# Attention and routed experts in one kernel: exponential scores of two heads on the two row halves of TensorE, one value bank by 512 queries, three maximum banks, the maxima split on GpSimd, fp32 down products

## The reference, cut to what matters

```python
q = (x @ Wq.T + bq); k = (x @ Wk.T + bk); v = (x @ Wv.T + bv)      # x: 2 x 1024 x 128, 16 heads of 8
scores = einsum('bqhd,bkhd->bhqk', q, k) * attn_scale[0]
scores = where(mask, -inf, scores)   # kept: keys of a later chunk of 64, and of the query's own chunk up to the query
attn = softmax(scores);  x = layernorm(x + (attn @ v) @ Wo.T + bo)
# experts: 32 of hidden size 64, top 6 of the best 4 of 8 groups, and one shared expert of hidden size 128
routed += combine[:, e] * ((silu(x @ gate_e.T) * (x @ up_e.T)) @ down_e.T)
x = layernorm(x + routed + shared)
```

## Time and profile before

| what | value |
|---|---|
| median of 3 runs | 520.54 us (520.14 to 521.09) |
| span of the profiled execution, first to last instruction | 514.3 us |
| what lies around the span, median less span | 6.2 us |
| projections, splits, values of V | 0 to 37.8 us |
| maxima of group 0 to the last maximum (start of L761 of group 7) | 38.9 to 276.2 us |
| first and last exponential product | 69.3 to 312.2 us |
| last value product | 317.4 us |
| first and last down product | 325.5 to 504.3 us |

### The profile page before, as it was taken

One profiled execution on the slowest core, in us unless ns is written; L12 is line 12 of the kernel. 1 busy time (PEld: TensorE's weight loads), 2 busy tenths in 40 slices (PEclk: granted clock), 3 DMA queues, 4 the chain that ended last, 5 costly groups with the idle time before them and its releaser, 6 DMA issues.

```text
span 514.3 us, 8899 instructions
## 1 busy us (share of the span) xinstructions
PE 468.9 (91%) x3212; PEld 259.2 (50%) x3212; DVE 402.1 (78%) x780; ACT 263.1 (51%) x375; POOL 216.8 (42%) x260
## 2 busy tenths in 40 slices
PE   5899799999999999999999997898988898899872
PEld 1474233444434444443434553686765576667651
DVE  7809977788887878788786457699889889968963
ACT  4510035666656676665576766444564464545440
POOL 9100033625345362544413323455644556655561
PEclk9955559999999999999999999899999999999996
DMA  4444110020211203020000000633222253452320
GB/s 138 154 145 134 59 34 15 7 88 20 73 39 31 66 19 83 26 65 32 3 2 3 1 1 2 138 109 92 83 82 82 83 112 96 120 135 83 102 82 20
DMA packets 23340, 34.22 MB, mean 67 GB/s; under 512 B 5121, under 2 KB 13186, under 8 KB 22530
## 3 DMA queue, kind: packets, MB, share of 16 engines
q1 hardware_dynamic: 23106, 33.41, 22.7%
q10 hardware_dynamic: 192, 0.26, 0.2%
HBM read 29.00 MB, written 4.46 MB: 65 GB/s over the span
## 4 chain that ended last, share of the span: by engine, by line
PE 59%; DVE 16%; issue 10%; POOL 10%; ACT 3%; DMA 2%; SPq 1%; DVEq 0%; POOLq 0%; ACTq 0%
PE ps L1082 15%; PE ps L1039 13%; PE ps L1064 12%; POOL hlo L615 8%; DVE mx L758 6%; DVE hh L983 3%; PE ps L1042 3%; DVE au L978 2%; PE ps L1013 2%; PE ps L1010 2%; PE ps L1149 2%; PE ps L1151 2%; PE ps L1150 2%; POOL rstd L588 1%; PE ps L1176 1%
## 5 line engine op out<-in xcount | busy, mean ns | idle before, releaser
L758 DVE TENSOR_REDUCE mx<-ps 128x1 f32<-128x512 f32 (+3 forms) x304 | 189.7, 660 | 45.4 <-PE ps L1042 37.6
L660 ACT ACTIVATE probs<-ps 128x1024 f32<-128x1024 f32 (+4 forms) x176 | 147.8, 869 | 110.8 <-PE ps L1064 110.4
L615 POOL TENSOR_TENSOR hlo<-hh,hhi 128x512 fp32r<-128x512 f32 x68 | 91.4, 1351 | 90.6 <-ACT hhi L715 85.3
L1039 PE MATMUL ps<-rows_k,rows_q 72*128 72x512 bf16 (+3 forms) x384 | 123.8, 365 | 2.1 <-DVE mx L758 0.9
L570 POOL TENSOR_SCALAR_AFFINE_SELECT probs<-probs 64x512 f32<-64x512 f32 x64 | 42.4, 662 | 127.1 <-ACT probs L660 126.1
L1082 PE MATMUL ps<-probs,Vg 128*32 128x256 f32 (+1 forms) x1280 | 92.9, 370 | 0.0
L1064 PE MATMUL ps<-rows_q,rows_k 99*128 99x512 bf16 (+3 forms) x384 | 92.3, 334 | 0.0
L1039 PEld LDWEIGHTS ps<-rows_k,rows_q 72*128 72x128 bf16 x384 | 37.5, 103 | 81.7 <-DVE mx L758 53.5
L983 DVE TENSOR_TENSOR hh<-rows_k,au 128x512 f32<-128x512 f32 x64 | 71.4, 1115 | 5.8 <-DMA rows_k<-weights 3.6
L726 ACT ACTIVATE sg<-ps 128x512 f32<-128x512 f32 x68 | 40.7, 598 | 55.7 <-PE ps L1151 54.1
L978 DVE TENSOR_TENSOR au<-ps,sg 128x512 f32<-128x512 f32 x64 | 43.7, 683 | 19.2 <-POOL hlo L615 10.5
(11 more groups left out here) (115 smaller groups left out, 479.5 us busy)
## 6 DMA issues: line engine op xcount, KB each, us to landing
rows_k<-weights SPq DMA_DIRECT2D x128, 128.0 KB, 3.0
w_raw<-in_unitT SPq DMA_DIRECT2D x17, 192.0 KB, 12.4
scratch<-oT SPq DMA_DIRECT2D x8, 384.0 KB, 2.9
rows_q<-scratch SPq DMA_DIRECT2D x8, 192.0 KB
rows_k<-scratch SPq DMA_DIRECT2D x8, 192.0 KB
xT<-in_xT SPq DMA_DIRECT2D x4, 256.0 KB, 4.4
rows_q<-scratch SPq DMA_DIRECT2D x8, 128.0 KB
rows_k<-scratch SPq DMA_DIRECT2D x8, 128.0 KB
```

Of the source, the lines that this page charges most:

```text
L615: pool.tensor_tensor(hlo[:, i % 2, :], hh[:, i % 2, :], hhi[:, i % 2, :], ALU.subtract).then_inc(hidden_low, 1)
L660: act.activation(dst, src, ACT.Exp).then_inc(exps_ready, 1)
L758: dve.tensor_reduce(mx[:, part, j:j + per, qt], src, AX.X, ALU.max).then_inc(max_read, 1)
L1039: mm = pe.matmul(bank(max_bank(g, n), m, at), q, rows_k[0:K_MAX, s, j * T + k0:j * T + k0 + m], start=True, stop=part == 1)
```

## The change

- **Two heads on row halves.** `rows_q` and `rows_k` hold heads 0 and 1 of a group at partitions 0 to 50 and heads 2 and 3 at 64 to 114. Score products contract over 48 or 51 rows and so take a 64-row tile of the array; an exponential unit issues the same product for both halves, one behind the other, into two banks. A maximum unit lies on one half, and successive units alternate between the halves. The mask becomes two products of 64 columns on the unit's own half.
- **Loads.** `load_rows` issues 12 transfers instead of 6, `store_max` 6 instead of 3. The zero and one fills of the slots shrink to one fill of ones in `rows_k`.
- **Values.** 12 blocks of up to 512 queries instead of 20 pieces of up to 256, all in bank 4, one half of the queries after the other; `probs` has four slots of one block.
- **Maxima.** Banks 5 to 7 instead of two banks (four in group 0). The transposed maxima are taken after unit 3 of the next group; ACT copies them to `tops`, GpSimd splits them in five operations. Groups have 40 units instead of 38.
- **Value bias.** The bias of V is added on GpSimd instead of by a one-row product; half of the V projections moves into the maxima of group 0.
- **Experts.** `hhi`, `hlo` and the split of the down weights go; `down` is one fp32 product (two instructions). The down weights come as one transfer behind `store_max(0)`.
- **Order.** The planner also plans GpSimd, and SP follows the same list. The bias of x is added by quarters.

```diff
-ROWS_QK = 48
-MROW = 96
-K_MAX = 72
-K_EXP = MROW + 3
+ROWS = 48
+K_EXP = ROWS + 3
+ROW_HALF = P // 2
+PAIRS = HG // 2
...
-            per = BANK // m if BANK % m == 0 else 1
-            for j in range(0, HG, per):
-                units.append(([(j + a, qt, k0, m, a * m) for a in range(per)], m, part))
+            heads = [(0, 1), (2, 3)] if 2 * m <= BANK else [(0,), (2,), (1,), (3,)]
+            units += [([(j, qt, k0, m, a * m) for a, j in enumerate(js)], m, part) for js in heads]
...
+BLOCKS = [(0, 7), (0, 3), (0, 6), (0, 2), (0, 5), (0, 1), (0, 4), (0, 0), (1, 7), (1, 6), (1, 5), (1, 4)]
+QH = T // BANK
+HALF = KT // QH
+SLOTS = 4
+def width(b):
+    qh, kt = BLOCKS[b]
+    return min(BANK, P * (kt + 1) - BANK * qh)
...
+        units += [(b, (0, 1), n)] if 2 * n <= BANK else [(b, (0,), n), (b, (1,), n)]
...
+TOP_AFTER = 3
+MSEQ = []
+for g_ in range(NG):
+    for n_ in range(NM):
+        MSEQ.append(("unit", g_, n_))
+        if g_ and n_ == TOP_AFTER:
+            MSEQ.append(("top", g_ - 1, 0))
+MSEQ.append(("top", NG - 1, 0))
+MAX_AT = {step: r for r, step in enumerate(MSEQ)}
+RING, RING0 = 3, 5
...
-    hop, rows_latency, load = 240, 5500, 6000
-    LEAD = 1.5
...
+    hop, rows_latency, load = 240, 3500, 6000
+    LEAD = 1.6
...
+                    for f in range(2):
+                        if reps is None:
+                            spans = ((0, 24, part[f]), (24, 16, part[f, 0:2]), (40, 8, part[f, 0]))
+                        else:
+                            spans = ((0, 24, part[f, 0:1].to_broadcast([3, D, PAIRS * T])),
+                                     (24, 16, part[f, 1:2].to_broadcast([2, D, PAIRS * T])), (40, 8, part[f, 2]))
+                        for at, n, src in spans:
+                            sp.dma_start(dst[ROW_HALF * f + at:ROW_HALF * f + at + n, s, :],
+                                         src).then_inc(rows_loaded[s], 16)
...
-                for h in range(3):
-                    sp.dma_start(rows_q[MROW + h:MROW + h + 1, s, :], mh[:, h, :]).then_inc(max_rows_loaded[s], 16)
+                for f in range(2):
+                    for h in range(3):
+                        at = ROW_HALF * f + ROWS + h
+                        sp.dma_start(rows_q[at:at + 1, s, :],
+                                     mh[PAIRS * KT * f:PAIRS * KT * (f + 1), h, :]).then_inc(max_rows_loaded[s], 16)
...
+            for what, g, n in pool_order:
+                if what == "w":
+                    load_unit(n)
+                elif what == "split":
+                    store_max(g)
+                    if g == 0:
+                        sp.dma_start(w_down[:, :, :], a["unitT"][:, :, 2 * P:]).then_inc(down_loaded, 16)
+                elif what == "mask" and n == NB - 1 and g < NG - NS:
+                    sp.wait_ge(exp_scores, NE * (g + 1))
+                    load_rows(g + NS)
...
+            def split_top(g):
+                pool.wait_ge(tops_copied, g + 1)
+                if g >= 1:
+                    pool.wait_ge(max_rows_loaded[(g - 1) % NS], 96 * ((g - 1) // NS + 1))
+                pool.tensor_scalar(mh[:, 0, :], tops[:, :], -1.0, None, ALU.mult).then_inc(max_split_steps, 1)
+                pool.wait_ge(max_split_steps, 3 * g + 1)
+                pool.tensor_tensor(mr[:, :], tops[:, :], mh[:, 0, :], ALU.add).then_inc(max_split_steps, 1)
+                pool.wait_ge(max_split_steps, 3 * g + 2)
+                pool.tensor_scalar(mh[:, 1, :], mr[:, :], -1.0, None, ALU.mult).then_inc(max_split_steps, 1)
+                pool.wait_ge(max_split_steps, 3 * g + 3)
+                pool.tensor_tensor(mr[:, :], mr[:, :], mh[:, 1, :], ALU.add).then_inc(max_rest, 1)
+                pool.wait_ge(max_rest, g + 1)
+                pool.tensor_scalar(mh[:, 2, :], mr[:, :], -1.0, None, ALU.mult).then_inc(max_split, 1)
...
-            def low_part(i):
-                pool.wait_ge(hidden_high, i + 1)
-                if i >= 2:
-                    pool.wait_ge(down_done, i - 1)
-                pool.tensor_tensor(hlo[:, i % 2, :], hh[:, i % 2, :], hhi[:, i % 2, :],
-                                   ALU.subtract).then_inc(hidden_low, 1)
...
+            def copy_tops(g):
+                act.wait_ge(tops_turned, g + 1)
+                if g >= 1:
+                    act.wait_ge(max_rest, g)
+                act.copy(tops[:, :], bank(max_bank(("top", g, 0)), P)[0:HG * KT, :]).then_inc(tops_copied, 1)
...
-                top = bank(TOP, P)[0:HG * KT, :]
-                dve.wait_ge(max_scores, NM * (g + 1))
-                dve.tensor_scalar(mh[:, 0, :], top, -1.0, None, ALU.mult).then_inc(max_split_steps, 1)
-                dve.wait_ge(max_split_steps, 3 * g + 1)
-                dve.scalar_tensor_tensor(mr[:, :], top, -1.0, mh[:, 0, :], ALU.mult,
-                                         ALU.subtract).then_inc(max_split_steps, 1)
-                dve.wait_ge(max_split_steps, 3 * g + 2)
-                dve.tensor_copy(mh[:, 1, :], mr[:, :]).then_inc(max_split_steps, 1)
-                dve.wait_ge(max_split_steps, 3 * g + 3)
-                dve.tensor_tensor(mh[:, 2, :], mr[:, :], mh[:, 1, :], ALU.subtract).then_inc(max_split, 1)
...
-                    dve.wait_ge(hidden_low, i - 1)
+                    dve.wait_ge(down_done, i - 1)
...
-                    mm = pe.matmul(bank(2 + n, P, t * P), ones[0:1, :], bvr[0:1, :], start=False, stop=True)
+                    mm = pe.matmul(bank(n, P, t * P), xT[:, tt * P:(tt + 1) * P], wv[:, :], start=True, stop=True)
...
+                if r >= RING:
+                    was, g_, n_ = MSEQ[r - RING]
+                    if was == "unit":
+                        pe.wait_ge(max_read, NM * g_ + n_ + 1)
+                    else:
+                        pe.wait_ge(tops_copied, g_ + 1)
...
-                    q = rows_q[0:K_MAX, s, j * T + qt * P:j * T + (qt + 1) * P]
-                    mm = pe.matmul(bank(max_bank(g, n), m, at), q, rows_k[0:K_MAX, s, j * T + k0:j * T + k0 + m],
-                                   start=True, stop=part == 1)
+                    f, p = ROW_HALF * (j // PAIRS), j % PAIRS * T
+                    mm = pe.matmul(bank(b, m, at), rows_q[f:f + ROWS, s, p + qt * P:p + (qt + 1) * P],
+                                   rows_k[f:f + ROWS, s, p + k0:p + k0 + m], start=True, stop=part == 1)
                     if part == 0:
-                        mm = pe.matmul(bank(max_bank(g, n), P, at), identb[:, :], mask_qk[:, :], start=False,
-                                       stop=True)
+                        for c in range(2):
+                            mm = pe.matmul(bank(b, CHUNK, at + c * CHUNK), pick[f:f + CHUNK, c, :],
+                                           mask_k[f:f + CHUNK, :], start=False, stop=c == 1)
...
-                cols = P * (kt + 1)
-                for a_ in range(per):
-                    j = j0 + a_
-                    base = (n % 2) * 2 * BANK + a_ * stride
-                    k = rows_k[0:K_EXP, s, j * T + kt * P:j * T + (kt + 1) * P]
-                    for c0 in range(0, cols, BANK):
-                        m = min(BANK, cols - c0)
-                        mm = pe.matmul(ps[:, base + c0:base + c0 + m], k,
-                                       rows_q[0:K_EXP, s, j * T + c0:j * T + c0 + m],
-                                       start=True, stop=True)
+                for a_, p in enumerate(pairs):
+                    for f in range(2):
+                        r = slice(ROW_HALF * f, ROW_HALF * f + K_EXP)
+                        mm = pe.matmul(bank((NE * g + n) % 2 * 2 + f, m, a_ * m),
+                                       rows_k[r, s, p * T + kt * P:p * T + (kt + 1) * P],
+                                       rows_q[r, s, p * T + qh * BANK:p * T + qh * BANK + m], start=True, stop=True)
...
-                m = min(PIECE, P * (kt + 1) - c0)
-                slot, c = PLACE[kt]
+                    if outputs_before(g, qh):
+                        pe.wait_ge(output_copied, outputs_before(g, qh))
+                pe.wait_ge(exps_ready, NE * g + EXPS_UP_TO[b])
+                if masked(b):
+                    pe.wait_ge(squares_masked, 2 * (NMASK * g + MASKS_UP_TO[b]))
+                m = width(b)
                 for j in range(HG):
-                    mm = pe.matmul(ps[STRIP * j:STRIP * (j + 1), 4 * BANK + c0:4 * BANK + c0 + m],
-                                   Vg[:, g % 2, kt, j, :], probs[:, slot, j * T + c + c0:j * T + c + c0 + m],
-                                   start=kt == KT - 1 and c0 % BANK == 0, stop=n + 1 in (UPPER_DONE, NV),
+                    mm = pe.matmul(ps[STRIP * j:STRIP * (j + 1), VALUES * BANK:VALUES * BANK + m],
+                                   Vg[:, g % 2, kt, j, :], probs[:, (NB * g + b) % SLOTS, j, 0:m],
+                                   start=kt == KT - 1, stop=b == HALF_END[qh],
...
-                w = slice(2 * P, 3 * P)
-                pe.matmul(bank(ACC), w_hi[:, u, w], hhi[:, i % 2, :], start=u == 0, stop=False)
```

(3 more changed lines are left out.)

503 lines of the change are left out of this document (254 added, 249 removed).

## The result

The changed kernel takes **491.5 us** (median of four runs, 491.3 to 492.0) against 520.8; the ratio is 0.9442, 95% interval 0.9427 to 0.9457. The forecast was 481 with a range of 460 to 508: the sign and the range held, and the median lies 10.5 us above the forecast.

What follows compares the result with a forecast made beforehand. PE was taken to set the attention period, 30.36 us a group, with a down-product chain in the expert loop. Start +1, steady attention -26, tail -4 and experts -10 gave -39 from 520.5: 481 us, range 460 to 508.

Steps and rivals of the forecast that it cites:

- The steady stretch: Attention groups 1 to 7: PE-bound period of 26.0 us a group, 4.4 less; six periods give -26 us.
- the tail: From the attention's last maximum to its last value product: 38 us instead of 42, -4.
- The start: Up to group 1's last maximum: SP's longer queue puts the first exponential at 73 instead of 69.3 us; +1.
- the experts: Expert loop: fp32 down product of 0.93 us, unit 2.32 us instead of 2.67, 67 units; -10 (bounds -5 and -15).
- mutual waiting: Steady attention: 1 us a group added because PE (25) and VectorE (22.9) share one fixed order over three banks.
- overlapping maxima: Steady attention, PE: opposite-half maxima overlap with neighbours; a third of the possible saving taken, 27.0 to 25 us a group.
- VectorE as the bound: Rival, steady attention: halves overlap fully, VectorE's reductions set 23.5 us a group; 466 us in all, chance 0.13.
- No packing: Rival, steady attention: halves do not run side by side or the order stalls; 495 to 508 us, chance 0.14.
- An unseen wait that eats the gain: Catch-all case, no place named: anything else, such as an unseen wait that eats all; chance 0.02.
- the forecast's own case: Steady attention PE-bound at 24.5 to 27.5 us a group, 470 to 494 us in all; chance 0.62.
- The rule of the Trainium skill: Start: activity alone releases the clock throttle, so 2.4 GHz returns some 5 us sooner; 476 us, given a tenth.
- The rival with narrow products: Rival, from 73 us on: products over 48 or 51 rows leave PE at 1.2 GHz; up to 613 us, chance 0.09.

Runs made afterwards that it cites:

- e3: Changed kernel with four row slots instead of three and expert weight loads issued two split steps ahead: 467.6 us.
- e12: Changed kernel with four row slots instead of three and expert weight loads issued one step ahead: 466.9 us.
- e5: e3 with maxima of wide blocks in head order 0, 1, 2, 3 instead of 0, 2, 1, 3: 466.7 us.
- e2: Changed kernel, still three row slots, with expert weight loads issued two split steps ahead: 504.1 us.
- e10: Changed kernel, still three row slots, with expert weight loads issued one step ahead: 494.9 us.
- e1: Changed kernel with four row slots instead of three, the fourth first loaded behind the stored maxima of group 0: 484.7 us.
- e6: e3 with each exponential product over rows 0 to 114, both halves at once, so that none run side by side: 496.4 us.
- e4: Kernel before the change with only the single fp32 down product, no hhi, hlo or down-weight split, attention as before: 502.9 us.
- e7: Changed kernel with 14 added fp32 identity products on PE before the first maximum of groups 5, 6 and 7: 489.6 us.

## Why the prediction was right in sign, and 10 us short

By stages, on the spans, counted from the last reduction of group 1 on (93.3 us before, 86.5 now), -24.3 in all:

| stage | forecast | measured |
|---|---|---|
| to the last maximum of group 1 | +1 | 93.3 to 86.5: -6.8 |
| six steady periods | -26 | 182.2 to 175.2: -7.0 |
| last maximum to last value | -4 | 41.9 to 48.0: +6.1 |
| to the first down product | 0 | 8.1 to 8.0: -0.1 |
| 67 expert units | -10 | 178.8 to 162.6: -16.2 |
| end | 0 | 10.0 to 9.7: -0.3 |

The range held in part by luck. The steady stretch missed by 19 us and the tail by 10, which alone make 481 + 29 = 510, outside the range. The start (7.8 better), the experts (6.2), the 4.2 us of the quick profiled execution and 0.4 elsewhere brought it back to 491.5.

**The steady attention: the step that failed.** The sum of PE's work, 25 us and 1 of mutual waiting, came out: 25.4 in e3, 25.1 in e12. Its credit of 2 us for overlapping maxima is not confirmed by e5, so the single terms need not be right. What failed is that nothing was priced for the reload of a slot. The text counted SP's 36 row transfers of the start and left out those that the change adds in each later group, 12 in place of 6, 7.7 us on SP. Before, PE was full in this stretch, so the reload cost nothing there. In the changed kernel, from a group's last exponential score to the first maximum in its slot it takes 14 us by VectorE's start, and the order was made for 6. With three slots a period cannot be under (a group's way from first maximum to last exponential score, plus 14) / 3. That way is 76.8 us here, and 65.5 in e3 (137.5 to 203.0), with four slots: (65.5 + 14.2) / 3 = 26.6, above PE's 25.4 already. And it feeds on itself: any wait inside it, masks too, delays the last score, thus the load, thus the next group's start, on a PE that does its steps in a fixed order. That is how e2 and e10 could take mask waits away and win nothing, and how the two cures together gave 24 us. Of the 24.5 us by which the six periods of the changed kernel exceed those of e12, 15.0 are waits, and 9.5 are PE's own products taking longer, which goes with the time at 1.2 GHz. That the loop closes is arithmetic on the five kernels of the table; that the fourth slot removes it is shown by e1, e3 and e12. Why the way is 80 us in e10 and 77 in the changed kernel is not settled.

**Mutual waiting and VectorE.** VectorE as the bound (chance 0.13) did not come: e6 shows PE full and 3.3 us slower. In e3 the two are near each other: 5.1 us of PE's waits are for VectorE. No packing (0.14) is refuted by e6 and by starts 0.01 us apart. An unseen wait that eats the gain had 0.02, and it was the one at work: with the clock's falls behind it, it ate 19 us of 26. The period of 29.2 us lies outside the forecast's own case of 24.5 to 27.5.

**The start: -6.8 instead of +1.** The first exponential ran at 69.9, not 73, and SP's queue did not hold the maxima's rows: SP stood on `wo` for 11.9 us, not 21, and was free at 60.3.

```profile
46.14 0.86 SPq L533 DMA_DIRECT2D x<-in_x  x1
47.03 11.85 SPq L534 DMA_DIRECT2D wo<-in_woT  x1
...
64.22 3.83 SPq L550 DMA_DIRECT2D rows_q<-mh  x6
```

The stores at 64.22 waited for the split. The forecast carried the 21.1 us of the earlier trace rows over as a constant, but the transfer left SP at nearly the same time, 58.9 us and 61.5 before, although it was issued 6.6 us later. That it waits for what stands in front of it in the queue is a reading; no run varied it. The price of a row transfer, 0.64 us, was right (2.00 / 3 is 0.67, but 7.7 us for 12 were measured). Of the 7.8 us by which the stage came out better, 3.1 are the earlier exponential and 4.9 the stretch behind it (16.6 us instead of 21.5): the clock was back at 76 us, 3 us after the first values at 73.05, where the forecast had about 85. The rule of the Trainium skill (TensorE: Matmul & The Clock Gate, Part 1), that activity alone releases the throttle, would have it earlier still, yet PE was nine tenths busy from 37 to 61 us and stayed at 1.2 GHz:

```profile
PE   6339979998698789798899997789999999999992
```

The rise came behind full-row products, as in the kernel before.

**The tail: +6.1 instead of -4.** The changed order leaves 1.6 groups of exponentials after the last maximum. The forecast had 30 us on ScalarE and 32 on PE, and took 38. It took 48 us in e3 as well (239 to 287), so the waits of the steady stretch are not to blame. From 262 to 310 us PE was busy 42.6 us. Its value products hold 19.4 of them and its exponential products 10.3, together 29.7 against the 27 priced. So 12.9 at least are for the steps of the output projection, the router and the first ups, which were put at 5. The other 5.4 us PE stood, and before, it stood 1.7 of 42. The mis-sized term is thus the projection steps, and short waits that were put at nothing.

**The experts: right mechanism, mis-sized.** PE at 333.6 us; the down product is a pair of instructions:

```profile
333.59 0.40 PE L1209 MATMUL ps<-x1hi,w_lo 128*128 128x512 f32 x1
333.83 1.02 PE L1235 MATMUL ps<-hh,w_down 128*128 128x512 f32 x2
```

The next product starts at 334.69, so it is 0.86 us, not 0.93; 67 x 0.07 is 4.7 us, and with 2 of stalls that never came this makes up the difference of 169.4 forecast and 162.6 measured. The 0.93 came from a record's length less 0.17; the lower of the forecast's two bounds by a value piece, 0.87, was the right one. e4 shows the same 17 us with the attention as before.

**The clock.** The rival with narrow products (chance 0.09) did not come: e12 runs the same products from 87 to 238 us at 2.4 GHz throughout. But the clock fell at holes, four times from 127 us on, 30.7 us in all, and this the forecast had at nothing. The Trainium skill (TensorE: Matmul & The Clock Gate, HAM oscillation) reckons the cost as half of the throttled time. By that rule 30.7 us at 1.2 GHz would cost 15. The runs show less: PE's time without waits is 9.5 us longer than in e12, and e7 took 13.6 us of it away for 1.9 us of the end. PE stood waiting for part of the time at 1.2 GHz anyway.
